# AdaLN transformer block on one core: when the modulation partition sums run in the QKV stage, which PSUM bank holds a third of unit 0's row maxima, and when the output weights' low halves are made

## The reference, cut to what matters

```python
mod = (_silu(L0_c) @ L0_wmod).reshape(L0_c.shape[0], 6, 1, -1)      # L0_wmod: 1024 x 6144
sa, ca, ga, sb, cb, gb = (mod[:, 0], mod[:, 1], mod[:, 2], mod[:, 3], mod[:, 4], mod[:, 5])
h = _layernorm(x, axis=-1) * (1 + ca) + sa
q = (h @ Wq.T).reshape(b, t, h_kv, g, d).transpose(0, 2, 3, 1, 4)   # 32 heads of 32
k = (h @ Wk.T).reshape(b, t, h_kv, d).transpose(0, 2, 1, 3)         # 8 heads of 32
v = (h @ Wv.T).reshape(b, t, h_kv, d).transpose(0, 2, 1, 3)
att = softmax(einsum('bhgqd,bhkd->bhgqk', q, k) / sqrt(d))
x = x + ga * (einsum('bhgqk,bhkd->bhgqd', att, v) @ Wo.T + bo)
h = _layernorm(x, axis=-1) * (1 + cb) + sb
x = x + gb * _L0_ffn_ref(h, w_gate, w_up, w_down)
```

## Time and profile before

| what | us |
|---|---|
| median of 3 runs | 3411.93 (3411.88 to 3412.88) |
| the profiled execution's own time | 3413.24 |
| its span, first to last instruction | 3411.6 |
| TensorE busy | 3359.1 |
| VectorE busy | 2253.6 |
| POOL busy | 1622.0 |
| ScalarE busy | 1582.8 |

### The profile page before, as it was taken

One profiled execution on the slowest core, in us unless ns is written; L12 is line 12 of the kernel. 1 busy time (PEld: TensorE's weight loads), 2 busy tenths in 40 slices (PEclk: granted clock), 3 DMA queues, 4 the chain that ended last, 5 costly groups with the idle time before them and its releaser, 6 DMA issues.

```text
span 3411.6 us, 45330 instructions
## 1 busy us (share of the span) xinstructions
PE 3359.1 (98%) x16999; PEld 2278.8 (67%) x16999; DVE 2253.6 (66%) x3764; ACT 1582.8 (46%) x2992; POOL 1622.0 (48%) x726
## 2 busy tenths in 40 slices
PE   7999999999999999999999999999999999999999
PEld 5788555555555555555555478888888888887887
DVE  5767887787777777777777488544444444444728
ACT  3211566676666666666666723212222212214544
POOL 1223789989989998899898800000000000001010
PEclk9999999999999999999999999999999999999999
DMA  6567655656565555555555655511111111004222
GB/s 238 193 201 221 166 107 115 120 111 127 107 127 110 112 118 114 124 110 120 119 108 117 142 170 176 171 32 31 31 30 31 31 31 31 25 30 142 95 72 90
DMA packets 197620, 370.35 MB, mean 109 GB/s; under 512 B 44288, under 2 KB 119552, under 8 KB 179008
## 3 DMA queue, kind: packets, MB, share of 16 engines
q0 software_dynamic: 39808, 204.24, 25.9%
q1 hardware_dynamic: 154176, 157.45, 16.5%
q10 hardware_dynamic: 3456, 6.29, 0.6%
HBM read 168.29 MB, written 64.87 MB: 68 GB/s over the span
## 4 chain that ended last, share of the span: by engine, by line
PE 84%; DVE 6%; DMA 4%; issue 2%; POOL 2%; ACT 1%; SPq 0%; ACTq 0%; DVEq 0%; POOLq 0%
PE att_scores L1186 14%; PE gu_gate_acc L1787 14%; PE gu_up_acc L1787 13%; PE att_scores_T L1200 13%; PE att_y_acc L1211 12%; PE wo_acc L1480 4%; PE down_acc L2120 4%; PE qkv_qk_acc L629 3%; PE down_acc L2151 2%; PE att_den_acc L902 2%; DMA att_exp_pair<-att_exp_pair 1%; POOL att_exp_pair L1012 1%; DMA qkv_wqkv_raw<-in_wmod 1%; DVE att_chunk_max L1110 1%; ACT qkv_h_affine L346 1%
## 5 line engine op out<-in xcount | busy, mean ns | idle before, releaser
L1110 DVE TENSOR_REDUCE att_chunk_max<-att_scores 128x1 f32<-128x512 f32 x1984 | 1212.9, 681 | 314.4 <-PE att_scores L1186 314.2
L1078 ACT ACTIVATE att_exp<-att_scores_T 128x512 f32<-128x512 f32 x2032 | 1028.6, 625 | 418.8 <-PE att_scores_T L1200 412.1
L1012 POOL TENSOR_TENSOR att_exp_pair<-att_exp 128x2048 f32<-128x2048 f32 x252 | 1186.7, 4776 | 13.7 <-ACT att_exp L1078 12.0
L1211 PE MATMUL att_y_acc<-att_exp,att_v_head 128*32 128x512 f32 x4096 | 494.3, 600 | 0.5 <-ACT att_exp L1078 0.5
L1644 POOL DMA_DIRECT2D inter_scratch<-gu_inter x84 | 45.2, 538 | 853.8 <-DVE gu_inter L1521 853.8
L1186 PE MATMUL att_scores<-att_kq,att_q_stack 96*128 96x512 f32 x768 | 313.6, 413 | 0.7 <-DVE qkv_qk_out_lo L442 0.3
L1186 PE MATMUL att_scores<-att_k_stack,att_q_stack 96*128 96x512 f32 x768 | 313.9, 411 | 0.0
L1200 PE MATMUL att_scores_T<-att_q_stack,att_kq 98*128 98x512 f32 x768 | 299.0, 408 | 2.3 <-DMA att_q_stack<-att_max_T_lo 2.3
L1200 PE MATMUL att_scores_T<-att_q_stack,att_k_stack 98*128 98x512 f32 x752 | 292.8, 412 | 4.4 <-DMA att_q_stack<-att_max_T_lo 3.9
L1709 ACT ACTIVATE gu_magnitude<-gu_value 128x512 f32<-128x512 f32 (+1 forms) x88 | 55.7, 633 | 511.6 <-DVE gu_value L1745 511.6
L1211 PEld LDWEIGHTS att_y_acc<-att_exp,att_v_head 128*32 128x32 f32 x4096 | 106.9, 109 | 236.9 <-ACT att_exp L1078 152.7
(11 more groups left out here) (250 smaller groups left out, 6090.0 us busy)
## 6 DMA issues: line engine op xcount, KB each, us to landing
att_exp_pair<-att_exp_pair POOLq DMA_DIRECT2D x128, 1024.0 KB, 7.4
att_q_stack<-q_scratch SPq DMA_DIRECT2D x72, 256.0 KB, 6.0
qkv_wqkv_raw<-in_wmod POOLq DMA_DIRECT2D x32, 512.0 KB, 4.5
shared_raw<-in_wd_t POOLq DMA_DIRECT2D x34, 256.0 KB, 3.0
qkv_x_tile<-in_x SPq DMA_DIRECT2D x16, 512.0 KB, 3.9
q_scratch<-qkv_qk_out_hi POOLq DMA_DIRECT2D x32, 256.0 KB, 3.7
q_scratch<-qkv_qk_out_lo POOLq DMA_DIRECT2D x32, 256.0 KB, 4.2
y_scratch<-att_y_out SPq DMA_DIRECT2D x32, 256.0 KB, 2.6
```

The source lines that it names most:

```text
L1012: nc.gpsimd.tensor_tensor(ps[PAIR_SLOT[j]][:], pr[2 * j % NP][:], pr[(2 * j + 1) % NP][:], ALU.add).then_inc(pair_done, 1)
L1078: nc.scalar.activation(pr[k % NP][:, h * NB:(h + 1) * NB], st_bank(u, GH * k + h)[:], ACT.Exp, scale=INV_SQRT_DH).then_inc(exp_done, 1)
L1110: nc.vector.reduce_max(cmax[c % 2][:, q:q + 1], turn_buffer(u, q)[:], AX.X).then_inc(sm_done, steps_done(u, q))
L1211: ins = nc.tensor.matmul(yp[h * DH:(h + 1) * DH, :], vg[c // QB % 2][:, k, :], pr[k % NP][:, h * NB:(h + 1) * NB], start=(k == 0), stop=(k ...
```

## The change

1. The sums of parts 1 and 2 and all that follows each stand one position later (SUM_AT = 1): the sum behind position 1, the transposes and the columns behind position 2. In block 2 the sum is then behind `transposes` of that position, in block 3 behind the four V tiles.
2. In block 2 no half is added at positions 0 and 1; positions 2 to 7 take one each, positions 8 and 9 five each (before: one each at 0 to 7, then four and four).
3. SyncE stores the rows of part 2, and waits for both stores, behind the loads of q0 and k0 instead of ahead of them.
4. The third bank of unit 0's row maxima is V bank vp[1] instead of modp. TensorE no longer waits for `mod_done` at q = 0 and waits for `v_evac` of 15 V tiles at q = 2.
5. POOL makes the low halves of Wo at positions 3 to 9 instead of 2 to 8.

```diff
-        HALVES = [0, 1, 2, 3, 4, 5, 6, 7, 8, 12, NHALF]
+        HALVES = {1: [0, 1, 2, 3, 4, 5, 6, 7, 8, 12, NHALF], 2: [0, 0, 0, 1, 2, 3, 4, 5, 6, 11, NHALF]}
+        SUM_AT = 1
...
-            return (tr[:, 0:NB], tr[:, NB:2 * NB], modp[:])[q % 3]
+            return (tr[:, 0:NB], tr[:, NB:2 * NB], vp[1][:])[q % 3]
...
-            return [(b - 1) * NHALF + i for i in range(HALVES[m], HALVES[m + 1])] if 1 <= b < NG else []
+            return [(b - 1) * NHALF + i for i in range(HALVES[b][m], HALVES[b][m + 1])] if b in HALVES else []
...
+            def store_rows(g):
+                sp.wait_ge(mod_rows, g + 1)
+                for j in ((0, 1), (2, 3))[g - 1]:
+                    sp.dma_start(mod_dram[g * GW + j * NB:g * GW + (j + 1) * NB].rearrange("(a n) -> a n", a=1),
+                                 rows[32 * j:32 * j + 1, :]).then_inc(row_stored, 16)
+
             for t in range(BT, TT):
                 load_x(t)
-                if t in (TT - 3, TT - 1):
-
-                    g = 1 if t < TT - 1 else 2
-                    sp.wait_ge(mod_rows, g + 1)
-                    for j in ((0, 1), (2, 3))[g - 1]:
-                        sp.dma_start(mod_dram[g * GW + j * NB:g * GW + (j + 1) * NB].rearrange("(a n) -> a n", a=1),
-                                     rows[32 * j:32 * j + 1, :]).then_inc(row_stored, 16)
-            sp.wait_ge(row_stored, 16 * 4)
+                if t == TT - 3:
+                    store_rows(1)
...
+            store_rows(2)
+            sp.wait_ge(row_stored, 16 * 4)
...
-                    if b == QB - 1 and MK <= m < MK + FT - 1:
-                        for k in ((0, 1) if m == MK else (m - MK + 1,)):
+                    if b == QB - 1 and MK < m < MK + FT:
+                        for k in ((0, 1) if m == MK + 1 else (m - MK,)):
                             wo_lo(k)
...
-                        if m == 0:
+                        if m == SUM_AT:
                             mod_rows_out(b - 1)
-                        if m == 1:
+                        if m == SUM_AT + 1:
                             mod_columns(b - 1)
...
-                    pe.wait_ge(mod_done, NG)
+                if q == 2:
+                    pe.wait_ge(v_evac, TT - 1)
...
-                    if b >= 2 and p == 0:
+                    if b >= 2 and p == SUM_AT:
                         pe.wait_ge(mod_done, b - 1)
                         modulation_sum(b - 1)
-                    if b >= 2 and p == 1:
+                    if b >= 2 and p == SUM_AT + 1:
                         modulation_T(b - 1)
```

## The result

The changed kernel takes 3418.57 us (median of 20 runs, 3413.77 to 3423.29) against 3411.66 us for the kernel before over the same number (3409.16 to 3418.31). The ratio is 1.0018, 95% interval 1.0011 to 1.0024: 6.1 us slower, between 3.8 and 8.2 (the two medians are 6.9 apart). On the base of the prediction (3411.93) that is 3418.1, at the top of the range, whose end was 3418.2; the forecast was +0.9. The profiled execution took 3415.89 us, the second shortest of the 20, and its span is 3414.2.

What follows compares the result with a forecast made beforehand. TensorE, busy 3359.1 of 3411.6 us, was taken as the bound, so only its waits could yield time. Terms -2.3 + 1.5 + 1.7 = +0.9 us gave 3412.8 us, range 3408.2 to 3418.2.

Steps and rivals of the forecast that it cites:

- The ceiling: TensorE's waits at the two partition sums, with the low clock, cost 7.1 us; the change can give back no more.
- Term A: Part 1's sum near 197 us: its wait becomes 2.3 us for the norm; -2.3 us, bounds -2.7 to -0.6.
- Term B: Part 2's sum: its wait goes, TensorE waits 4.7 us for K at the first score tile; +1.5 us, -2.0 to +8.5.
- by the row I leave it at 0: q0's early loads, 2.6 us of transfers, delay the halves by nothing, since the DMA engines are not full there.
- Term C: Clock falls after the wait of nearly 5 us for K; +1.7 us, between 0 and twice that.
- the rival that I gave 0.13: q0's early loads stretch part 2's last halves; half 15 ends at 281 or later; 3415.3 to 3419.8 us; chance 0.13.
- The V bank and the low halves of Wo: The V bank for row maxima and POOL's later low halves of Wo cost nothing.
- The limits at which I would have called the prediction wrong: Wait for K missing or above 8 us, or naming V's bank; attention beginning more than 5 us from 350.4.
- That both waits go: Norm ends before 197.4 and K lands before 287.5; -7.1 us, 3404.8 us; chance 0.05.
- That K comes early: Loads and stores land at short values; wait 1.2 to 3 us, clock stays; 3407.6 to 3411 us; chance 0.22.
- The clock low behind both waits: Clock falls behind the norm's wait as well as K's; +1.7 us, 3414.5 us; chance 0.13.
- The slower one, q0's early loads: q0's early loads stretch the last halves and K lands at 295 to 299; 3415.3 to 3419.8 us; chance 0.13.

Runs made afterwards that it cites:

- e7: The kernel of e6 with the norm of x tile 12 done early, between halves 13 and 14; ratio 0.9976 to the kernel before.
- e3: The changed kernel with VectorE's norm of x tile 12 moved between halves 14 and 15 of part 1; ratio 1.0004 to the kernel before.
- e8: The kernel before with only part 1's sum, rows, transposes and columns one position later, and block 2's first halves with them; ratio 1.0006 to the kernel before.
- e2: The changed kernel with block 2's halves one at position 1, two at 2, one each at 3 to 7, four each at 8 and 9; ratio 0.9998 to before.
- e6: The changed kernel with part 2's last four halves put behind tile 30's way out, in VectorE's and POOL's lists; ratio 0.9990 to the kernel before.
- e1: The changed kernel with SyncE issuing q0's loads only once part 2's last half is added; ratio 1.0007 to the kernel before.
- e5: The changed kernel with e1's wait, e2's table of halves and e3's early norm together; ratio 0.9983 to the kernel before.
- e4: The kernel before with only the V bank for unit 0's row maxima and the later low halves of Wo; ratio 1.0003 to the kernel before.

## Why the prediction was right in kind and short in size

**The ceiling.** I said that the two sums cost 7.1 us and that no more could be had. e7, with none of these waits, has a stage 7.9 us shorter; half of the 0.8 more is one of the two later waits of 0.5 us for a norm, which is gone too; the rest I can't place. The runs put e7 at 8.2 us (5.1 to 11.6). Right.

**Term A (part 1), -2.3.** The wait went to the norm, as worked out from the earlier trace rows, 2.8 us instead of 2.3. e3 shows that it was that norm alone. The exchange of waits is right. The size is not shown, though the stretch from V tile 7 to V tile 11 is 1.9 shorter in this trace. A wait of 2.6 us was exchanged for one of 2.8, so most of the 1.9 is the low clock (1.7) that the kernel before had behind the sum and this execution had not behind the norm. Five traces have the sum moved and the norm in its old place, and they differ by just that: 75.2 (the change) and 75.9 (e8) with the clock high behind the norm's wait, 76.8 (e2) and 76.2 (e6) with 3.4 us of low clock, 77.9 (e1) with 6.8. Their mean is 0.7 below the 77.05 of the kernel before, which is the bound of -0.6 that I gave for a clock that falls. And e8's times leave no room for a gain above 1.0 us. That the clock stays high behind this wait was a draw of one execution, and -2.3 took it as given.

**Term B (part 2), +1.5.** The chain was right link by link but for one: K wanted 24.3 us behind the copy of V tile 11 (24.0 worked out), K there 14.0 us behind the last half (13.9 worked out; the landing was 5.4 and I had taken 5.5). The link that failed is the end of the last half: 14.8 us behind V tile 11's copy by my sum, 17.6 in the trace. So the wait is 7.3 and not 4.7, and the term is +4.1 for K, with 0.35 for the row transposes.

**The step that failed** is "by the row I leave it at 0", of q0's loads going out 15 us earlier. Half 13's load landed after 8.5 us against a median of 4.4, 4.1 more; e1, which only holds those loads back, brings the landings to 5.4 at most and the last half 3.3 us forward. I had argued from a mean busy share of 0.87 that room was left. That was the wrong reading. Of the 2.6 us that the 0.75 MB take at the rate of the earlier trace rows, the free 0.13 of 6 us could hold an estimated 0.8, and the rest had to push something back. The link was 2.8 us longer than worked out. The change against e1, which differ in q0's loads alone, gives 3.3, and e2 against e5, which differ in q0's loads and in the norm, 4.2: both more than 2.6. The rule of the Trainium skill that I had weighed (Trainium Kernel Development and Optimization, Key Constraints) says that transfers of all queues run on the same 16 engines and interleave. The delayed half loads agree with it.

**Term C (the clock), +1.7.** The low stretch came, and was twice as long as the one priced: 6.8 us, of which 4.2 behind the wait. From the first score tile to attention the changed kernel takes 2.3 us more; less the 0.35 of the row transposes it is +2.0. Near in size; the 2.6 us of the low stretch that lay inside the wait cost nothing of their own.

**Sum.** -1.9 + 4.1 + 0.35 + 2.0 = +4.6 instead of +0.9; of the 3.7 missing, 2.9 are K, 0.4 part 1 and 0.3 the clock. That is the sum of one trace; the runs say +6.1, and the 1.5 between them is not placed. Term A at its -0.7 instead of -1.9 would give 1.2 of it, and the clock over the 20 executions points the same way, but no trace shows it. The outcome is the rival that I gave 0.13, in the mechanism and near the point that I named for it (half 15 at 281 or later on the clock of the kernel before: 278.5 + 2.6 = 281.1). So the time fell inside the range by luck as much as by judgement: 3418.1 against an end of 3418.2, reached through the rival and not through the sum. The V bank and the low halves of Wo, put at nothing, show no wait in e4; in time it allows up to 4 us.

**The signs.** There was no wait at the sum (line 555, now 558). The others were foretold and measured thus: the wait for the norm 2.3 and 2.8, the wait for K about 5 and 7.3 with the clock low around it, q0's loads issued near 261 and at 260.9, the last half at 276 to 277 and at 278.5. The limits at which I would have called the prediction wrong were not passed, though the wait for K came near its 8 us. Attention began at 354.2, 3.8 us away from 350.4, with a limit of 5.

**The rivals.** That both waits go is refuted by the trace; it takes e7's two moves, or e5's three. That K comes early is refuted. The clock low behind both waits did not occur in the profiled execution, and did in e1 and e2, which wait at the same two places. For the other 19 executions of the change it is open, and their lower mean clock speaks for it in some of them. The slower one, q0's early loads, is what happened.

## What to carry to other kernels

When work is pushed back to make a wait vanish, look in the same engine's list for what stands behind it: here the store that the next stage's first load reads back from HBM. Two repairs of the wait for K worked: to time the filler better (e5), and, with fewer edits, to put the item with the longest tail ahead of it (e6). That tail was 14 us here: 2.3 us of a memset and a short gap ahead of it, then 12 us for out of PSUM, store and load back. And a transfer that is released early is not free because its data are early: here, in a stretch whose DMA engines had been 0.87 busy without it, it delayed a load of another queue by 4 us, and only what waited for that load shows whether this matters. Last, a gain that consists of a clock that stayed high in one execution has to be looked for in several traces or in the times.

## What the runs showed of the hardware

A wait of TensorE of 2.3 to 3.4 us may or may not cost clock: over the profiled executions of this study it was followed by a low stretch of 3.4 us, or of 6.8, or by none (before 2.61: 3.4, 2.81: none; the change 2.84: none; e1 2.66: 6.8; e2 2.27: 3.4; e4 3.35: 3.4, 3.23: none; e6 2.32: 3.4; e8 2.61: none, 2.97: 6.8). Every wait for K (2.6, 4.9, 5.9 and 7.3 us) had 6.8 us of low clock around it, even the shortest. I have no explanation of that last regularity; four executions do not settle it, and e1's wait of 2.66 us for the norm and e8's of 3.0 us at the sum had the long stretch too. e8's:

```profile
269.00:276.00 7.00, 6.50 (x19) 3.90 (x20) 4.10 (x5) 0.00 (x0) 1.09 (x2) 0.52 0.20 75
```

With 0.75 MB of q0 beside them, half loads of 0.5 MB took 8.1 and 8.8 us in e2 where 4.4 is the median: some 4 us more each, against the 2.6 us that the added bytes take at the rate of the earlier trace rows.
